# Causal attention: the softmax weights added up before their sums are taken, in place of a matmul per key tile

## The reference

```
# in layer 1's feed-forward part: heads of 64, masked before the softmax
scores = where(mask, scores, -inf) / sqrt(K);  p = softmax(scores);  out = p @ v

# in layer 3's cross-attention, part a1: heads of 32, masked after the softmax
a = softmax(q @ k.T * 32**-0.5);  a = a * (key not later than query);  o = a @ v
```

## Time and profile before

| | |
|---|---|
| runs, median (lowest, highest) | 1885.97 us (1880.84, 1887.44) |
| the profiled execution | 1887.49 us, its span 1885.0 us |
| busy PE / DVE / ACT / POOL | 1515.1 / 1074.3 / 642.5 / 146.3 us |
| mean granted TensorE clock | 0.885 |

### The profile page before, as it was taken

One profiled execution on the slowest core, in us unless ns is written; L12 is line 12 of the kernel. 1 busy time (PEld: TensorE's weight loads), 2 busy tenths in 40 slices (PEclk: granted clock), 3 DMA queues, 4 the chain that ended last, 5 costly groups with the idle time before them and its releaser, 6 DMA issues. The chain is left out here.

```text
span 1885.0 us, 22777 instructions
## 1 busy us (share of the span) xinstructions
PE 1515.1 (80%) x8376; PEld 699.1 (37%) x8376; DVE 1074.3 (57%) x2713; ACT 642.5 (34%) x901; POOL 146.3 (8%) x169
## 2 busy tenths in 40 slices
PE   1797779985677889998979997978988479994874
PEld 0332344431223344446433323354437223343342
DVE  4696445457946667763553962646454557744345
ACT  1365332213324023332424663422221145542431
POOL 2000010000000500001000000000000103321000
PEclk9899679995969889998997997998986789997797
DMA  4000000011000010000010000000010000000000
GB/s 196 0 1 1 1 1 1 1 51 81 1 1 1 1 45 1 1 1 1 0 57 42 1 1 1 1 1 1 1 67 1 1 0 1 2 1 0 1 1 11
DMA packets 4077, 27.18 MB, mean 14 GB/s; under 512 B 384, under 2 KB 2432, under 8 KB 2944
## 3 DMA queue, kind: packets, MB, share of 16 engines
q1 hardware_dynamic: 2912, 25.21, 3.4%
q10 hardware_dynamic: 1056, 0.52, 0.1%
HBM read 25.21 MB, written 0.52 MB: 14 GB/s over the span
## 5 line engine op out<-in xcount | busy, mean ns | idle before, releaser
L630 DVE TENSOR_REDUCE maxima<-banks 128x1 f32<-128x512 f32 (+4 forms) x640 | 362.8, 603 | 109.6 <-PE banks L501 102.2
L760 ACT ACTIVATE big<-banks 128x1024 f32<-128x1024 f32 (+2 forms) x320 | 294.3, 960 | 283.4 <-PE banks L544 113.1
L529 PE MATMUL banks<-big 32*128 32x512 f32 (+6 forms) x1280 | 232.5, 614 | 17.4 <-DVE big L651 12.6
L501 PE MATMUL banks<-big 32*128 32x77 bf16 (+6 forms) x1024 | 152.4, 295 | 21.9 <-ACT big L236 6.1
L1221 DVE TENSOR_TENSOR big<-big,banks 128x512 f32<-128x512 f32 (+1 forms) x116 | 79.7, 687 | 151.7 <-PE banks L1134 146.3
L565 PE MATMUL banks<-big,v_heads 128*9 128x512 f32 (+7 forms) x1024 | 159.5, 569 | 6.1 <-ACT heads_out L695 3.2
L344 POOL TENSOR_TENSOR rstd<-mean_var,minus_half 128x4 f32<-128x4 f32 x46 | 46.9, 1020 | 1504.9 <-DVE mean_var L319 1504.9
L1196 ACT ACTIVATE big<-banks 128x512 f32<-128x512 f32 (+1 forms) x116 | 69.1, 596 | 177.8 <-PE banks L1133 177.7
L1164 PE MATMUL banks<-big,moe_weights 128*128 128x512 f32 (+1 forms) x232 | 118.9, 597 | 3.0 <-ACT big L1204 2.6
L501 PEld LDWEIGHTS banks<-big 32*128 32x128 bf16 (+1 forms) x1024 | 56.4, 97 | 171.5 <-DVE maxima L630 84.8
L529 PEld LDWEIGHTS banks<-big 32*128 32x128 f32 (+3 forms) x1280 | 73.1, 178 | 67.4 <-ACT big L760 26.0
(11 more groups left out here) (379 smaller groups left out, 2220.7 us busy)
## 6 DMA issues: line engine op xcount, KB each, us to landing
moe_weights<-in_moe SPq DMA_DIRECT2D x1, 4864.0 KB, 14.8
moe_weights<-in_moe SPq DMA_DIRECT2D x1, 4768.0 KB, 21.8
moe_weights<-in_moe SPq DMA_DIRECT2D x1, 3264.0 KB, 10.7
moe_weights<-in_l3x SPq DMA_DIRECT2D x1, 3072.0 KB, 10.2
late_weights<-in_l2x SPq DMA_DIRECT2D x1, 2048.0 KB, 7.8
moe_weights<-in_l SPq DMA_DIRECT2D x1, 1234.0 KB, 13.3
rows<-in_rows SPq DMA_DIRECT2D x1, 1152.0 KB, 8.1
late_weights<-in_turned SPq DMA_DIRECT2D x1, 1152.0 KB, 17.1
```

Of the source, the lines that this page charges most:

```text
L501: last = nc.tensor.matmul(RING[n % NR][:, x * klen:x * klen + last_key(t)], q[rows, t * P:(t + 1) * P], ks[rows, 0:last_key(t)], start=Tru ...
L529: last = nc.tensor.matmul(SC[pair % 2][0:size, j % 2, n0:S], ks[rows, i * P:i * P + size], q[rows, n0:S], start=True, stop=turned)
L630: nc.vector.tensor_reduce(dst, src, AX_X, ALU.max).then_inc(ring_free.up(), 1)
L760: nc.scalar.activation(E[pair % NEP][0:size, :, n0:S], SC[pair % 2][0:size, :, n0:S], ACT.Exp, scale=scale).then_inc(exp_ready.up(), 1)
```

## The change

Denominators are no longer summed by PE for each key tile. For mask "causal" and "future" with more than one key tile (`added_up`), the weight tiles of a group are first added elementwise, in SBUF, and PE then multiplies by the ones once a group and head (`added_sums`), after the second round of the next group's work. The additions stand in `add_weights`:

- Layer 1 (one pair a round): all on POOL. For a group's second tile a copy of the first 128 columns and an addition of the rest; then one addition each for the third and fourth tile, over ever fewer columns. The total lies in the buffer that layer 3 uses for masked weights.
- Layer 3 (two pairs a round): the first pair on POOL, behind the two mask multiplications of its round; the second pair on DVE, in round r+1 between move_negmax and invert_sums. Each is a 128x1024 float32 addition, three a group. There are now eight E buffers.

The sums have their own copy out of PSUM (`move_sums`). In layer 1 two groups share one turning and inverting of sums (`per_batch` = 2), and turn_sums stands four rounds behind a batch's last round instead of three (`turn_after`), spread_inverses six instead of five. Layer 1's raw scores run two rounds ahead beyond a group (`raws_ahead`), and its negmax is taken one round earlier. The high part of negmax is now one scalar_tensor_tensor (-2m + m) in place of a tensor_scalar.

```diff
-    nkt, klen, pairs, NEP = len(key_tiles), sum(key_tiles), HB // 2, 4
+    nkt, klen, pairs = len(key_tiles), sum(key_tiles), HB // 2
-    per_batch = 2 if halved and nkt == 1 else 1
+    added_up = not turned and nkt > 1
+    raws_ahead = 2 if halved and nkt > 1 else 1
+    lead = U + raws_ahead * per_round
+    per_batch = 2 if halved else 1
-    later = 5 if nkt > 1 else 4
+    turn_after = 4 if added_up else 3
+    later = turn_after + (2 if nkt > 1 else 1)
+    E, EM = c.E + (c.E_more if added_up and pairs == 2 else []), c.EM
+    NEP, NEM = len(E), len(EM)
+    added_up_in = [c.added] if pairs == 1 else c.added_pairs
...
+    def additions(r):
+        return r // nkt * (nkt - 1) + max(r % nkt, 1)
...
+    def add_weights(eng, program, r, x, done):
+        g, n = r // nkt, r % nkt
+        if n == 0:
+            return
+        total = added_up_in[x]
+        new, first = E[(r * pairs + x) % NEP], start(tile(r))
+        program.wait_ge(exp_ready.sem, exp_ready.at(r * pairs + x + 1))
+        if n == 1:
+            if g:
+                program.wait_ge(den_ready.sem, den_ready.at(g))
+            old = E[((r - 1) * pairs + x) % NEP]
+            if first:
+                eng.tensor_copy(total[:, :, 0:first], old[:, :, 0:first])
+        else:
+            old = total
+            program.wait_ge(done.sem, done.at(g * (nkt - 1) + n - 1))
+        eng.tensor_tensor(total[:, :, first:], old[:, :, first:], new[:, :, first:], ALU.add).then_inc(done.up(), 1)
+
+    def added_sums(pe, g):
+        pe.wait_ge(added.sem, added.at((g + 1) * (nkt - 1)))
+        if pairs == 2:
+            pe.wait_ge(added_too.sem, added_too.at((g + 1) * (nkt - 1)))
+        if g == 0 and halved:
+            pe.wait_ge(cleared.sem, cleared.at(1))
+        if g >= per_batch and g % per_batch == 0:
+            pe.wait_ge(den_moved.sem, den_moved.at(g // per_batch))
+        for j in range(HB):
+            at = 64 * (g % 2) + 32 * j if halved else 32 * j
+            last = nc.tensor.matmul(DEN[at:at + 32, :], c.ones[:, 0:32], added_up_in[j // 2][:, j % 2, :], start=True, stop=True)
+        last.then_inc(den_ready.up(), 1)
...
     def sums(pe, r):
+        if added_up:
+            return
...
-        seq(dve, dve_step, nc.vector.tensor_scalar(hi, m, -1.0, None, ALU.mult))
+        seq(dve, dve_step, nc.vector.scalar_tensor_tensor(out=hi, in0=m, scalar=-2.0, in1=m, op0=ALU.mult, op1=ALU.add))
...
# PE, round r
-                if summed(r - 3) is not None:
-                    turn_sums(pe, summed(r - 3))
+                if added_up and ended(r - 2) is not None:
+                    added_sums(pe, ended(r - 2))
+                if summed(r - turn_after) is not None:
+                    turn_sums(pe, summed(r - turn_after))
...
# ACT, before an exponential that takes a used buffer
+                        if added_up:
+                            s = added_too if pair % pairs else added
+                            act.wait_ge(s.sem, s.at(additions((pair - NEP) // pairs)))
...
# DVE, round r, between move_negmax and invert_sums
+                if added_up and pairs == 2 and 0 <= r - 1 < R:
+                    add_weights(nc.vector, dve, r - 1, 1, added_too)
...
# POOL
+            for r in range(R if added_up and pairs == 1 else 0):
+                add_weights(nc.gpsimd, pool, r, 0, added)
...
+                if pair % pairs:
+                    add_weights(nc.gpsimd, pool, pair // pairs, 0, added)
```

More of the change, by code:

```diff
@@ L464, in ahead @@
     def ahead(r):
-        first = (r + nkt + 1) * per_round
+        first = (r + nkt + raws_ahead) * per_round
         soon = list(range(first, min(first + per_round, NU)))
@@ L469, in last_use @@
     def last_use(r):
-        return r + 2 if halved and r % 2 == 0 else r + 1
+        return r + 2 if halved and not added_up and r % 2 == 0 else r + 1
+    def additions(r):
+        return r // nkt * (nkt - 1) + max(r % nkt, 1)
     def place(g):
@@ L567, in values @@
                 nc.tensor.matmul(out[:, 0:i * P], vop(b, HB * k + j, i), e[:, 0:i * P], start=first, stop=False, skip_group_check=True)
-        if turned or halved and r % 2 == 0:
+        if turned or halved and (added_up or r % 2 == 0):
             last.then_inc(value_ready.up(), 1)
+    def add_weights(eng, program, r, x, done):
[27 more added lines that the diff above has]
+        last.then_inc(den_ready.up(), 1)
     def sums(pe, r):
@@ L666, in invert_sums @@
             return
[L667 to L677, removed]
+        rc = c.RC[:, s % 2]
+        nc.vector.reciprocal(rc, tr[:, :, :, 0]).then_inc(ring_free.up(), 1)
+        dve.wait_ge(ring_free.sem, ring_free.at(n + 1))
         for x in range(per_batch):
@@ L691, in move_out @@
         act.wait_ge(value_ready.sem, value_ready.at((g + 1) * nkt))
+        if added_up:
+            nc.scalar.copy(place(g), OV[:, :]).then_inc(out_moved.up(), 1)
+            return
         if s >= 2:
@@ L700, in move_out, with move_sums @@
         last.then_inc(out_moved.up(), 1)
+    def move_sums(act, s):
+        act.wait_ge(den_ready.sem, den_ready.at((s + 1) * per_batch))
+        if s >= 2:
+            act.wait_ge(ring_free.sem, ring_free.at(sums_turned[s - 2] + 1))
+        nc.scalar.copy(OT[:, s % 2, :], DEN[:, :]).then_inc(den_moved.up(), 1)
     with nc.Block() as block:
@@ L705, in _ @@
             made, first = 0, 0
-            while first < U + per_round or made < len(projections):
-                wanted = needs[groups[first // U]] if needs and first < U + per_round else 0
+            while first < lead or made < len(projections):
+                wanted = needs[groups[first // U]] if needs and first < lead else 0
                 upto = min(max(wanted, made + (first > 0)), len(projections))
@@ L711, in _ @@
                 made = upto
-                for u in range(first, min(first + 2, U + per_round)):
+                for u in range(first, min(first + 2, lead)):
                     raw_scores(pe, u)
@@ L749, in _ @@
                 empty(act, project_bank(n)).then_inc(project_free.up(), 1)
-            for r in range(R + 2):
+            for r in range(R + 3):
                 if ended(r - 2) is not None:
                     move_out(act, ended(r - 2))
+                if added_up and summed(r - 3) is not None:
+                    move_sums(act, summed(r - 3))
                 if r >= R:
@@ L766, in _ @@
                 nc.vector.memset(OV[:, :] if turned else DEN[:, :], 0.0).then_inc(cleared.up(), 1)
-            for u in range(min(U + per_round, NU)):
+            for u in range(min(lead, NU)):
                 n = reduce_max(dve, u)
@@ L773, in _ @@
                 soon, rest = ahead(r)
-                if next_group(r) is not None:
-                    negmax(dve, next_group(r), n)
+                if next_group(r + raws_ahead - 1) is not None:
+                    negmax(dve, next_group(r + raws_ahead - 1), n)
                 turn_first = mask == "causal" and next_group(r) is not None
@@ L782, in _ @@
                     move_negmax(dve, next_group(r))
[L783 to L784 removed]
+                if added_up and pairs == 2 and 0 <= r - 1 < R:
+                    add_weights(nc.vector, dve, r - 1, 1, added_too)
+                if summed(r - turn_after) is not None:
+                    invert_sums(dve, summed(r - turn_after))
                 for u in rest:
@@ L2029, in decoder @@
         c.EM = [EM[:, i * 2 * P:(i + 1) * 2 * P].rearrange("p (x t) -> p x t", x=2) for i in range(4)]
+        c.added = EM[:].rearrange("p (x t) -> p x t", x=2)
+        c.added_pairs = [c.big3((4 + x) * TOK, TOK).rearrange("p (x t) -> p x t", x=2) for x in range(2)]
+        c.E_more = [ap.rearrange("p (x a) f -> p x (a f)", x=2) for ap in (c.XN[:], c.total[:])]
+        c.E_more += [ap.rearrange("p (x t) -> p x t", x=2) for ap in (c.XT[:], c.big3(6 * TOK, TOK))]
         c.OT = c.sb("heads_out", [P, 2 * S])[:].rearrange("p (z t) -> p z t", z=2)
```

19 lines of the change are left out of this document (11 added, 8 removed).

## The result

The changed kernel takes 1937.2 us (median of 4 runs, 1935.76 to 1938.76) against 1885.65: 1.0275 times the time before, 95% interval 1.0257 to 1.0292. The forecast was 1914 with 1935 at the upper end, so the direction held and the size did not: +51.5 us where +28 was said, and 2.2 us beyond the stated range. The profiled execution took 1938.76 us, its span 1936.9.

What follows compares the result with a forecast made beforehand. PE was taken to bound layer 1, PE and DVE together layer 3. 1887.5 - 10.5 (layer 1) + 38.5 (layer 3: 33, 1.5, 4) = 1915.5 profiled, 1914 us as median; range 1877 to 1935.

Steps and rivals of the forecast that it cites:

- PE's sums lie beside DVE's reduces: Layer 3: sums of nearly 1 us fill time PE would wait for DVE; removing them shortens a round some 0.2 us.
- DVE and POOL take turns: Layer 3: additions, masks and negmax block each other at SBUF; +5.5 us a group taken, 33 over six periods.
- The walk: Layer 3's four rounds followed in order of time: 18.8 us a group without collisions, 22.8 with them, against 17.2.
- DVE's busy share: Layer 3: predicted sign that DVE would be busy above 90% of the time.
- The reason for negmax's waiting: Layer 3: negmax's two instructions now both read two SBUF operands, so they contend with POOL's SBUF reads and block.
- Layer 1, 10.5 us a group, -10.5 in all: Layer 1: period 10.5 us instead of 11.19, 0.7 saved a group over 15 periods, ends of the stage at nothing.
- The round-by-round figure: Layer 1: walking the four rounds gave 9.3 us and 1.2 for turning and spreading, 10.5 a group.
- the clock: Layer 3 rival: PE's pauses lower the clock, a further 1.5 us a group, 1926 us in all; chance 0.1.
- The ends: Layer 3's first and last groups, outside the six mid-stage periods: +1.5 us and +4 us.

Runs made afterwards that it cites:

- no_adds: Changed kernel with both sets of layer 3 additions (POOL's and DVE's) and the waits for them left out: layer 3 period 16.92 us, whole 1880.97 us.
- filled: Changed kernel with twice 10 needless bf16 products a group in PE's two layer 3 pauses: period 22.44 us, clock 1.00, 15.6 us off the whole.
- hi_scalar: Changed kernel with negmax's high part by a tensor_scalar (one SBUF input) as before: first part 1729 ns, layer 3 periods the same to 0.1 us.
- no_pool_adds: Changed kernel with POOL's additions in layer 3 left out, DVE's kept: layer 3 period 20.68 us (19.1 to 22.3), clock 0.83.
- no_dve_adds: Changed kernel with DVE's additions in layer 3 left out, POOL's kept: layer 3 period 23.31 us, clock 0.72.

## Why the prediction was wrong in size, step by step

- *PE's sums lie beside DVE's reduces.* Right: 0.28 us for three products (no_adds), against 0.2 a round for some rounds.
- *DVE and POOL take turns.* Right, with its places: negmax from 1.9 us into round 3, a mask between its parts, the addition behind POOL's next. The walk said 22.8 us, the kernel at full clock shows 22.44, some 0.25 of it the filling. DVE's additions with only masks to meet were said to give 18.8 and gave 19.08. Over no_adds DVE's alone cost 2.2 us, POOL's alone 1.9, both together 5.5. That was the part of the forecast with the widest range, and it came out; over six periods, 33 said and 30.5 measured at full clock. One sign missed: DVE's busy share was to be above 90%, and it is 75% (111.44 of 148 us), in filled 85% (112.45 of 132.21).
- *The reason for negmax's waiting.* Half wrong (hi_scalar): an instruction with one input waited as well.
- *Layer 1, 10.5 us a group, -10.5 in all.* Measured 10.72, and -6.05 by layer 3's start. The round-by-round figure was good: from the first copy to the last it is -9.40 (155.88 against 165.28). The stage's start (first copy 1.4 us later, 0.7 of it already there when the stage begins) and its drain (1.9 us given back) I had cost at nothing.
- *The step that failed: the clock.* "Chance 0.1", "a further 1.5 us a group", kept out of the sum as a rival. It was no rival but a consequence of the forecast's own pauses: the walk had PE standing still 3.7 and 2.5 us a group, and then priced all the rounds behind them with rows at full clock. By filled it was 24.60 - 22.04 = 2.56 us a period, 15.4 us over six and 15.6 of the whole (17.1 between the two profiled spans). 1914 with it is 1930. The pauses themselves were shorter than said, 2.4 and 1.3 to 2.0 us.
- *The ends.* Said +1.5 and +4, measured +2.5 and +7.3, and 2.2 more behind the stage. The last group had POOL's last mask waiting behind an addition of 2.33 us, PE waiting 4.5 us for it, and its last products at the lower clock. From the last copy to the stage's end it is 20.4 us before, 27.7 changed, 27.0 in filled and 22.2 in no_pool_adds: 5.5 of the 7.3 go with POOL's additions, and filling, which stops with the last negmax, hardly helps. What the clock costs behind that point no run shows.

Of the account of the 51.9 us, layer 3's sharing and load at full clock are 6 x (22.04 - 16.95) = 30.5, the clock 15.4 in the same periods, ends 12.0, layer 1 -6.05. The forecast had 33, nothing, 5.5 and -10.5, in all 28: the clock is 15.4 of the 23.9 us between, the ends 6.5, layer 1 4.5, and layer 3's periods gave 2.5 back.

## What to carry to other kernels

Before moving work off the busiest engine, look at one period in order of time: if its next instruction then waits for another engine's, the saving is already spent. Work moved to POOL is not beside DVE's: price each small DVE instruction on the critical chain at the length of the POOL instruction that may be running, and give it a round of lead, or keep that work away. And where a forecast contains pauses of PE, price what follows them at the lower clock in the sum itself. Products put into a pause to keep the clock up are free only while they are shorter than the pause; look where the next instruction starts.

## What the runs showed of the hardware

- A DVE tensor_scalar of 128x16 with one SBUF input took 1729 ns beside POOL's 2.34 us addition, nearly the same as the form with two inputs (1.76 us), against 0.20 in the earlier trace rows; the reduces from PSUM kept their 683 ns beside it. The Trainium skill, "SBUF — State Buffer", section "Who interferes with whom", says that the later of two contending instructions blocks until the first is done; the ends of the rows above agree (0.08 and 0.10 us behind POOL's end). The same section names copy and tensor_scalar among the instructions that can run in a mode in which they contend with GpSimd, which would cover this one and the copy of the earlier trace rows; no run here shows in which mode they ran.
- It goes the other way too: masks of 0.73 us on POOL took 1.49 when DVE's addition had begun 0.4 to 0.6 us earlier, as in this stretch of the changed kernel in order of time:

```profile
1654.22 1.49 DVE L600 TENSOR_TENSOR big<-big 128x1024 f32<-128x1024 f32 x1
...
1654.81 1.49 POOL L864 TENSOR_TENSOR masked_weights<-total,key_later 128x256 f32<-128x256 f32 x1 [0.18 <-ACT total L817]
```

- What short pauses of PE cost through the clock. In no_dve_adds PE waited about 2.4 us a group ahead of turn_negmax, the granted clock over the stage was 0.72, and of 7.1 us a period only 1.9 were left once those pauses held work.
